# The flags of a stencil's four corners: one logical and over a hand-written access pattern in place of two comparisons

## The chip, the cores and the metric

The kernel runs on one NeuronCore of a Trainium2 chip. The metric is the device time of one execution in microseconds (us), lower is better. Beside the time there is a profile of one execution: a record of every instruction on TensorE (PE, and PEld for its weight loads), VectorE (DVE), ScalarE (ACT), GpSimd (POOL) and SyncE (SP), with starts, durations and what each waited for.

## The reference

The reference is a block of three parts on an input of 4 images of 32 x 32 pixels and 128 channels: a deformable convolution, an attention over the 1024 tokens of each image, and a mixture of experts with two experts for each image. Only the first part touches the change. Cut to that:

```python
offset = x1 @ off_w + off_b                      # 8 groups x 9 points x (x, y) for each pixel
mask = softmax((x1 @ mask_w + mask_b).reshape(N, H, W, 8, 9), -1)
loc = ref + grid * 1.0 + offset / norm           # where each of the 9 points is read
samples = bilinear_sample(img, 2.0 * loc - 1.0)  # four corners of the pixel cell, zero outside
out = (samples * mask).sum(-1)                   # 9 points, weighted
x = x + out @ out_w + out_b                      # then attention and experts
```

## The kernel before

The image rows are worked on in eight chunks of four rows; a chunk has all four images in the 128 partitions, and 4 rows x 8 groups = 32 row-groups for each partition. The nine bilinear reads of a row-group are written as one stencil of 7 x 7 weights: each point q = (kx, ky) puts an outer product of five "hat" weights in y and five in x at its place (ky, kx) in the 7 x 7 window. The hats lie in `hats` [128, 2, 288, 5]: axis 0 is x, axis 1 is y, then 32 row-groups x 9 points, then five taps. The y hats are multiplied by the softmax weight (`weigh_hats`, L1539).

A 7 x 7 stencil would have 49 taps. The four corner taps are left out: the kernel works with 45 (`NEAR`), and where a corner's weight isn't zero, that point counts as "far" and is fetched one by one by GpSimd. So for each row-group and each of the four corner points (kx, ky in {0, 2}) a flag says whether both the outermost x hat and the outermost y hat of that point are above zero. These flags are `at_corner` [128, 32, 2, 2], bf16. They are made on VectorE in `corners` (L1541 to L1551). TensorE sums them over the partitions, together with signs of the offsets, in `count_far` (L894 to L907, the flags in L903); the counts go to a list of far points (`list_far`, L1642) and to GpSimd.

The order of the work on VectorE is written out by hand. After a first part for chunk 0, `turn(k, ...)` runs for k = 0 to 6: it multiplies the shifted rows of chunk k with its stencil (`products`, L1656, 26 instructions for a chunk, each of 1024 or 512 elements for a partition), and between these products it prepares chunk k+1: the softmax (L1510 to L1529), `weigh_hats`, `corners`, and `stencils`, which for the points q = 0 to 8 makes an outer product (L1588) and adds it into the stencil (L1597). For 10 of the 32 row-groups the addition is done by TensorE instead (`sum_point`, L921), and since all nine points use one buffer `outer`, the outer product of point q >= 2 waits until TensorE has summed point q-1 (L1587, semaphore `outer_read`).

TensorE goes through the taps of chunk k one by one (`add_up`, L934, four transposing matmuls for each tap, waiting for `prod_done`), and between them it has nine convolution steps of chunk k+2 (L864), `count_far` (L902 to L905), the point sums (L921), the offsets of chunk k+2 (L856) and the output projection of chunk k-1 (L953 to L956). The buffer `prod` has seven slots, freed by `prod_free`. At the end of a turn ScalarE copies TensorE's point sums into the stencil (L600), and the first product of the next chunk waits for that.

There are eight calls of `corners`: one ahead of the turns for chunk 0, and one in each of the seven turns. In a turn it stands between `weigh_hats` (it waits for its result) and the outer product of point 0; it also waits for the far counts of the chunk before (`far_mm`).

## Time and profile before

| | |
|---|---|
| device time, three runs | 670.16 us median (669.46 to 671.59) |
| profiled execution | 669.48 us, of which 667.6 us from the first to the last instruction |
| granted TensorE clock, mean | 0.968 |
| TensorE matmul busy | 601.7 us (90%) |
| VectorE busy | 550.1 us (82%) |
| ScalarE busy | 235.1 us (35%) |
| GpSimd busy | 316.1 us (47%) |

In the profile a line L12 is line 12 of the kernel. A group of instructions is shown as line, engine, operation, output <- inputs, number, busy time and mean duration. "Idle before" is the time in which the engine stood still just before the instruction, with what ended it. The clock that the profile shows for TensorE is a share of 2.4 GHz: 1.00 is 2.4 GHz and 0.50 is 1.2 GHz. Matmul ends are modelled by the profile. The seven turns lie between 64.3 and 394.0 us; the attention and the experts follow them.

### The profile page before, as it was taken

Reading aid. Unit: us, or ns where it says so; the run is one execution under the profiler, and the core shown is the slowest. Engines: PE = TensorE matmul, PEld = TensorE weight load, DVE = VectorE, ACT = ScalarE, POOL = GpSimd, SP = SyncE. Lnnn points to the kernel's source line nnn. Section 1 sums busy time; section 2 is a strip of 40 time slices with the busy share of each in tenths; the row PEclk is TensorE's granted clock in tenths of the full one; section 3 lists DMA queues with packets and bytes.
Section 4 is the critical chain, followed back from the end, with each engine's and each line's share of the span. In section 5 each row is a group of like instructions: output and inputs, shape, how many; then the busy total and the mean of one; then the engine's idle time right before and its main releaser. Section 6 shows DMA issues by size and latency. Waiting matters only on the chain.

```text
span 667.6 us, 11041 instructions
## 1 busy us (share of the span) xinstructions
PE 601.7 (90%) x3634; PEld 444.3 (67%) x3634; DVE 550.1 (82%) x1028; ACT 235.1 (35%) x351; POOL 316.1 (47%) x408
## 2 busy tenths in 40 slices
PE   5989979979989989899797789999999999979995
PEld 4566656657667667576585567777777777765774
DVE  4668998999999999999999989757767766654877
ACT  6063504405307116126044000344454444415331
POOL 7604775786688588748578700202212211215222
PEclk9789989989989989989997999999999999999998
DMA  7087502103003007000000000000000000004111
GB/s 187 18 325 241 163 0 81 35 2 111 1 3 112 1 2 278 1 1 2 1 2 3 0 1 1 0 2 0 1 1 1 1 1 1 0 9 120 48 33 47
DMA packets 26243, 30.75 MB, mean 46 GB/s; under 512 B 5573, under 2 KB 18325, under 8 KB 26197
## 3 DMA queue, kind: packets, MB, share of 16 engines
q1 hardware_dynamic: 24094, 29.77, 13.6%
q0 software_dynamic: 1408, 0.36, 0.6%
q8 instruction: 29, 0.48, 0.3%
q14 instruction: 18, 0.14, 0.1%
q10 hardware_dynamic: 694, 0.01, 0.1%
HBM read 25.07 MB, written 5.05 MB: 45 GB/s over the span
## 4 chain that ended last, share of the span: by engine, by line
PE 58%; DVE 27%; issue 10%; ACT 3%; DMA 1%; DVEq 0%; POOL 0%; SPq 0%; ACTq 0%; POOLq 0%
DVE prod L1656 12%; PE banks L934 11%; PE banks L1061 9%; PE pair L1041 8%; DVE outer L1588 5%; PE pair L1129 4%; PE banks L1051 4%; PE pair L864 4%; PE banks L1167 4%; PE pair L856 2%; PE banks L921 2%; PE banks L956 2%; DVE stencil L1597 2%; DVE hats L1539 2%; ACT hats L624 1%
## 5 line engine op out<-in xcount | busy, mean ns | idle before, releaser
L934 PE MATMUL banks<-ident,prod 128*128 128x128 f32 x1440 | 203.6, 282 | 34.8 <-DVE prod L1656 33.7
L934 PEld LDWEIGHTS banks<-ident,prod 128*128 128x128 f32 x1440 | 165.4, 143 | 91.2 <-DVE prod L1656 64.9
L1656 DVE TENSOR_TENSOR prod<-shifted,stencil 128x1024 f32<-128x1024 f32 (+1 forms) x208 | 218.0, 1082 | 5.2 <-ACT stencil L600 3.5
L1412 POOL TENSOR_TENSOR rstd_now<-mv_now,neg_half 128x2 f32<-128x2 f32 x32 | 22.9, 716 | 127.4 <-DVE mv_now L1704 127.4
L864 PE MATMUL pair<-xg,dw_diag 128*128 128x512 f32 x144 | 74.6, 620 | 1.4 <-DVE xg L1466 1.4
L1307 POOL DMA_INDIRECT got<-padded,cell_now x44 | 57.8, 1314 | 19.0 <-issue 10.1
L1061 PEld LDWEIGHTS banks<-shifted 128*128 128x128 f32 x512 | 60.2, 192 | 8.1 <-issue 6.1
L1061 PE MATMUL banks<-shifted 128*128 128x128 f32 x512 | 63.3, 277 | 2.3 <-ACT shifted L740 1.4
L1588 DVE TENSOR_TENSOR outer<-hats 128x800 f32<-128x800 f32 x56 | 55.7, 995 | 6.2 <-PE banks L921 6.2
L1041 PE MATMUL pair<-shifted 128*128 128x512 f32 x128 | 60.6, 596 | 0.1
L1719 DVE TENSOR_REDUCE neg_max<-pair 128x1 f32<-128x1024 f32 x32 | 39.2, 1224 | 23.1 <-PE pair L1041 22.0
L624 ACT ACTIVATE hats<-off,tap_bias 128x576 f32<-128x576 f32 (+1 forms) x40 | 49.9, 1345 | 0.8
L735 ACT ACTIVATE shifted<-pair,neg_max 128x1024 f32<-128x1024 f32 x32 | 35.7, 1114 | 32.8 <-DVE neg_max L1719 32.7
L1597 DVE TENSOR_TENSOR stencil<-stencil,outer 128x550 f32<-128x550 f32 x56 | 41.6, 743 | 2.0
L646 ACT ACTIVATE xg<-banks 128x512 f32<-128x512 f32 (+1 forms) x8 | 4.8, 598 | 104.4 <-PE banks L941 104.4
L921 PE MATMUL banks<-outer,ident 128*128 128x250 f32 x116 | 37.4, 405 | 3.2 <-DVE outer L1588 3.2
L1724 DVE COPY shifted<-banks 128x512 f32<-128x512 f32 x32 | 22.0, 689 | 15.3 <-PE banks L1051 15.3
L1418 POOL TENSOR_TENSOR res<-res,bias_all 128x256 f32 x16 | 11.7, 728 | 46.2 <-DVE xg L1710 46.2
L1051 PE MATMUL banks<-ident,shifted 128*128 128x128 f32 x256 | 33.2, 273 | 0.3 <-ACT res L702 0.3
L1041 PEld LDWEIGHTS pair<-shifted 128*128 128x128 f32 x128 | 21.8, 190 | 15.9 <-issue 15.3
L864 PEld LDWEIGHTS pair<-xg,dw_diag 128*128 128x128 f32 x144 | 24.4, 201 | 11.4 <-issue 11.4
L1129 PE MATMUL pair<-shifted,stage 128*128 128x512 f32 x64 | 29.3, 597 | 2.3 <-DMA stage<-in_L_ffn_W_dram 2.3
(260 smaller groups left out, 957.3 us busy)
## 6 DMA issues: line engine op xcount, KB each, us to landing
shifted<-padded SPq DMA_DIRECT2D x42, 256.0 KB, 4.1
shifted<-padded SPq DMA_DIRECT2D x14, 640.0 KB, 8.2
res<-in_x_dram SPq DMA_DIRECT2D x4, 512.0 KB, 6.2
padded<-stage SPq DMA_DIRECT2D x4, 512.0 KB, 11.1
stage<-in_L_ffn_W_dram SPq DMA_DIRECT2D x16, 128.0 KB, 2.2
out_dram<-res SPq DMA_DIRECT2D x16, 128.0 KB, 1.8
got<-padded,cell_now POOLq DMA_INDIRECT x44, 2.9
padded<-stencil SPq DMA_DIRECT2D x2, 228.0 KB, 2.6
```

The costliest lines, as they stand in the source:

```text
L624: own(sc.activation(hats[:, :, :, t].rearrange("p a (r g) -> p a r g", r=ROWS), off[:, bass.ds(k % OFFS, 1), :, 0:2 * GP].rearrange("p s r ...
L864: mm = pe.matmul(conv_bank.rearrange("c (r a) -> c r a", r=ROWS), dw_diag[:, t, :], src, start=(t == 0), stop=(t == 8))
L921: pe.matmul(summed.rearrange("p (g a b) -> p g a b", a=WIN, b=WIN)[:, :, ky:ky + TAPS, kx:kx + TAPS], ident[:, :], src, start=False, stop= ...
L934: mm = pe.matmul(acc_of(c, r), prod[:, slot, r * G:(r + 1) * G, :].rearrange("p g c -> p (g c)"), ident[:, :], is_transpose=True, start=(t ...
L1041: mm = pe.matmul(pair[s][:, h * 512:(h + 1) * 512], keyed[:, bass.ds(i * P, P)], normed_t[:, bass.ds((i // TILES) * TOK + h * 512, 512)], ...
L1051: mm = pe.transpose(bank[h][:, m * P:(m + 1) * P], probs[:, s, (4 * h + m) * P:(4 * h + m + 1) * P], ident[:, :])
L1061: mm = pe.matmul(bank[2][:, 0:C], probs_t[:, m * P:(m + 1) * P], normed[:, bass.ds((i // TILES) * TILES + m, 1), :].rearrange("p t c -> p ...
L1129: pe.matmul(pair[j][:, (f % 2) * 512:(f % 2 + 1) * 512], w1_sel[:, 2 * (q // 2) + j, (f % 2) * P:(f % 2 + 1) * P], normed2_t[:, q * 512:(q ...
L1307: gp.indirect_dma_start(out=got[:, j, a, :], out_offset=None, in_=table, in_offset=bass.IndirectOffsetOnAxis(ap=cell_now[:, j, a:a + 1], a ...
L1588: ve.tensor_tensor(to if q == 0 else outer[:, :, :, :], hy[:, :, q, :].unsqueeze(3).to_broadcast(full), hx[:, :, q, :].unsqueeze(2).to_bro ...
L1597: own(ve.tensor_tensor(to, to, outer[:, 0:DIRECT, :, :], ALU.add))
L1656: ins = ve.tensor_tensor(prod[:, dx:dx + n, :, :], shifted[:, dx:dx + n, bass.ds(((c % HALF) * ROWS + dy) * G, ROWS * G), :], stencil_of[: ...
```

## The change

In `corners`, two instructions are replaced by one. Before, for each of the two point columns kx a SCALAR_TENSOR_TENSOR of 64 elements (32 row-groups x 2 point rows) compares the x hat with zero and the result with the y hat: (hx <= 0) < hy, which is one where both are above zero. After, one TENSOR_TENSOR of 128 elements takes the logical and of the x hats and the y hats. The two point columns and two point rows have different steps in `hats` (in x 34 and 10 elements, in y 30 and 14), which the pattern helper of the language doesn't give in one slice; so a small function writes the access pattern by hand. The output is the same [128, 32, 2, 2] of bf16, now written in one piece. The waits ahead of it and the semaphore behind it stay as they are.

```diff
+        def outermost(axis, per_column, per_row):
+            first = hats[:, axis, :, :].rearrange("p (g q) t -> p g (q t)", q=PTS)[:, :, 0:1]
+            return bass.AP(tensor=first.tensor, offset=first.offset,
+                           ap=[first.ap[0], first.ap[1], [per_column, 2], [per_row, 2]])
...
-                at = hats[:, :, :, :].rearrange("p a (g q) t -> p a g (q t)", q=PTS)
-                for kx in range(2):
-                    x0, y0 = (2 * 3 * TAPS + TAPS - 1) * kx, 2 * 3 * TAPS * kx
-                    last = ve.scalar_tensor_tensor(at_corner[:, :, kx, :], at[:, 0, :, x0:x0 + 2 * TAPS + 1:2 * TAPS], 0.0,
-                                                   at[:, 1, :, y0:y0 + 3 * TAPS:2 * TAPS + TAPS - 1], ALU.is_le, ALU.is_lt)
+                last = ve.tensor_tensor(at_corner[:, :, :, :], outermost(0, 2 * 3 * TAPS + TAPS - 1, 2 * TAPS),
+                                        outermost(1, 2 * 3 * TAPS, 2 * TAPS + TAPS - 1), ALU.logical_and)
                 last.then_inc(corners_done, 1)
```

On VectorE, in the first turn, the stretch around the flags stands so before the change (row: line, operation, output <- inputs, shape, semaphores waited for):

```order
L1529 TENSOR_TENSOR off<-mask,row_sum 128x4x72 [waits dve]
L1656 TENSOR_TENSOR prod<-shifted,stencil 128x512 [waits prod_free]
L1539 TENSOR_TENSOR hats<-hats,off 128x1440 [waits hats_done,dve]
L1549 SCALAR_TENSOR_TENSOR at_corner<-hats 128x32x2 [waits dve,far_mm]
L1549 SCALAR_TENSOR_TENSOR at_corner<-hats 128x32x2
L1588 TENSOR_TENSOR stencil<-hats 128x32x5x5 [waits dve,stencil_clear]
```

The same stretch of VectorE in the changed kernel, whose lines are numbered a little higher:

```order
L1534 TENSOR_TENSOR off<-mask,row_sum 128x4x72 [waits dve]
L1658 TENSOR_TENSOR prod<-shifted,stencil 128x512 [waits prod_free]
L1544 TENSOR_TENSOR hats<-hats,off 128x1440 [waits hats_done,dve]
L1551 TENSOR_TENSOR at_corner<-hats 128x128 [waits dve,far_mm]
L1590 TENSOR_TENSOR stencil<-hats 128x32x5x5 [waits dve,stencil_clear]
```

Nothing has moved: in this place and in the seven others two rows have become one, with the waits of the first. The order on the other engines is the same.

## Rows read from the trace of the kernel before

**Rows 1.** The page's costliest groups: taps on TensorE and products on VectorE.
```profile
L934 PE MATMUL banks<-ident,prod 128*128 128x128 f32 x1440 | 203.6, 282 | 34.8 <-DVE prod L1656 33.7
L1656 DVE TENSOR_TENSOR prod<-shifted,stencil 128x1024 f32<-128x1024 f32 (+1 forms) x208 | 218.0, 1082 | 5.2 <-ACT stencil L600 3.5
```

**Rows 2.** Windows, turns 0, 2, 4, 5, 6: length, busy PE, PEld, DVE, ACT, POOL; PEclk.
```profile
64.29:111.61 47.32, 41.41 (x236) 29.15 (x235) 45.06 (x53) 16.92 (x18) 30.00 (x42) 0.93 0.23 74
...
158.81:206.01 47.20, 43.19 (x263) 31.34 (x262) 44.93 (x54) 15.76 (x18) 34.01 (x35) 0.96 0.14 41
...
253.57:301.25 47.68, 43.21 (x263) 31.25 (x261) 45.57 (x53) 15.73 (x18) 32.03 (x40) 0.96 0.26 98
301.25:347.11 45.86, 41.37 (x259) 29.66 (x258) 45.16 (x54) 15.72 (x18) 33.06 (x39) 1.00 0.01 2
347.11:394.00 46.89, 36.46 (x246) 28.59 (x245) 44.64 (x53) 10.27 (x12) 29.28 (x33) 0.93 0.02 2
```

**Rows 3.** Groups of VectorE by shape: count, then busy us, mean ns, idle before.
```profile
L1588 DVE TENSOR_TENSOR outer<-hats 128x800 f32<-128x800 f32 x56 | 55.7, 995 | 6.2 <-PE banks L921 6.2
...
L1500 DVE SCALAR_TENSOR_TENSOR gate<-gate,conv 128x512 f32<-128x512 f32 x8 | 5.5, 682 | 4.5 <-ACT conv L591 4.5
...
L1466 DVE TENSOR_SCALAR xg<-xg,gn_v 128x864 f32<-128x864 f32 x4 | 4.1, 1117 | 0.0
...
L1549 DVE SCALAR_TENSOR_TENSOR at_corner<-hats 128x64 bf16<-128x64 f32 x16 | 3.8, 280 | 1.3 <-DVE hats L1539 1.2
...
L1513 DVE TENSOR_TENSOR mask<-off,row_max 128x288 f32<-128x288 f32 x8 | 3.6, 456 | 0.0
...
L1837 DVE TENSOR_SCALAR stage<-stage,weight_all 128x256 f32<-128x256 f32 x8 | 2.4, 345 | 0.0
...
L1466 DVE TENSOR_SCALAR xg<-xg,gn_v 128x160 f32<-128x160 f32 x4 | 1.5, 440 | 1.2 <-POOL gn_v L1227 1.2
...
L1784 DVE TENSOR_SCALAR route<-route,route_s 4x8 f32<-4x8 f32 x1 | 0.2, 219 | 0.0
...
L1794 DVE SCALAR_TENSOR_TENSOR route<-route 4x8 f32<-4x8 f32 x1 | 0.2, 154 | 0.0
```

**Rows 4.** VectorE in order of time (start, duration): chunk 0, turns 1, 2, 6.
```profile
54.82 0.99 DVE L1612 TENSOR_TENSOR prod<-hats 128x800 f32<-128x800 f32 x1 [1.72 <-PE banks L921]
...
128.70 0.99 DVE L1588 TENSOR_TENSOR outer<-hats 128x800 f32<-128x800 f32 x1
...
152.37 0.99 DVE L1588 TENSOR_TENSOR outer<-hats 128x800 f32<-128x800 f32 x1 [0.85 <-PE banks L921]
...
169.64 0.47 DVE L1549 SCALAR_TENSOR_TENSOR at_corner<-hats 128x64 bf16<-128x64 f32 x2 [0.18 <-DVE hats L1539]
170.02 0.98 DVE L1588 TENSOR_TENSOR stencil<-hats 128x800 f32<-128x800 f32 x1
...
176.00 0.98 DVE L1588 TENSOR_TENSOR outer<-hats 128x800 f32<-128x800 f32 x1
...
364.23 1.03 DVE L1588 TENSOR_TENSOR outer<-hats 128x800 f32<-128x800 f32 x1
```

**Rows 5.** TensorE in order of time: point sums and waits of the same turns.
```profile
128.01 0.59 PE L921 MATMUL banks<-outer,ident 128*128 128x250 f32 x2
...
151.68 0.59 PE L921 MATMUL banks<-outer,ident 128*128 128x250 f32 x2
...
175.23 0.59 PE L921 MATMUL banks<-outer,ident 128*128 128x250 f32 x2
...
182.59 2.23 PE L934 MATMUL banks<-ident,prod 128*128 128x128 f32 x16 [1.21 <-DVE prod L1656]
...
362.56 1.04 PE L921 MATMUL banks<-outer,ident 128*128 128x250 f32 x2
```

**Rows 6.** Windows of TensorE, in turns 2 and 5: length, busy, granted clock.
```profile
191.00:195.00 4.00, 4.00 (x19) 0.57 0.04 4
...
330.00:343.00 13.00, 11.38 (x77) 1.00 0.00 1
```

## The prediction

> **What bounds the kernel now.** I read the page first: its costliest groups are the taps on TensorE and the products on VectorE, and each waits for the other: TensorE stood idle 33.7 us for VectorE's products, VectorE hardly at all in front of a product [rows 1]. Both belong to the seven turns, so the turns were cut out as windows [rows 2]. A turn takes 45.9 to 47.7 us and VectorE is busy 44.6 to 45.6 us of it. It is the fuller engine, and the instructions that the change touches stand in its stream. Eight times 2 flags instructions take 16 x 280 ns [rows 3], under 4.5 us in all. So this is a question of a fraction of a microsecond for each turn, and whether it arrives at the end depends on what else is nearly late at that place.
>
> That was read from the order of time in turn 2. The pair of flags instructions starts at 169.64, the next instruction at 170.02 [rows 4]: the pair holds VectorE for 0.38 us. From there VectorE runs without a gap to point 2's outer product at 176.00. That one needs TensorE's sum of point 1, which stands at 175.23 and lasts 0.59, so until 175.82 [rows 5]. How long after such a sum VectorE can start is seen where it did wait: the sum at 151.68 ends at 152.27 and the outer product behind it starts at 152.37 [rows 4, 5], 0.10 us later. So at 176.00 only 0.08 us are free. TensorE works without a gap through its convolution steps before that sum, and it was released by the first products of the turn, ahead of the flags. **A VectorE that comes earlier to this place will meet TensorE's sum.** Behind it things are loose again: TensorE stands 1.21 us for a product at 182.59 [rows 5].
>
> **The change, part by part.** *Removed:* eight pairs of 64-element instructions. Each pair costs 0.38 us from its start to the next start. With 280 ns an instruction this says that the next one starts about 0.09 us before the end of the one before it (0.28 - 0.19).
>
> *Added:* eight instructions of 128 elements, a form that the trace doesn't have. Three rows bound it.
> - Dense: a TENSOR_TENSOR of 800 elements takes 995 ns, one of 288 takes 456 [rows 3], so 1.05 ns for an element and 153 ns fixed. At 128 elements this gives 288 ns, and to the next start 0.20 us. Saving: 0.38 - 0.20 = 0.18 us a turn.
> - With the price for scattered elements that the old form pays. Dense SCALAR_TENSOR_TENSORs take 154 ns at 8 elements and 682 at 512 [rows 3], so 64 dense elements would take 213. The flags take 280, 67 ns more. If this is paid for each element (1.05 ns more), the new one takes 288 + 128 x 1.05 = 422 ns, to the next start 0.33. Saving: about 0.05 us a turn.
> - The same 67 ns paid once for an instruction: 288 + 67 = 355 ns, to the next start 0.27. Saving: 0.11 us.
>
> Which? The two forms of the input's normalisation (L1466) step 16 bytes from element to element: 440 ns at 160 and 1117 at 864, 0.96 ns for an element. The dense TENSOR_SCALARs take 219 ns at 8 and 345 at 256, 0.51 for an element [rows 3]. So scattered elements cost more one by one, not once, and the flags' steps are wider still, both before and after. I take the second row, **0.05 us saved in each turn**, and keep 0.18 as the upper end. The lower end is below nothing: one instruction as long as the two old ones without their overlap, 0.56 - 0.09 = 0.47, loses 0.09 a turn; nothing in the trace excludes it, though it would need a price for an element that no row shows.
>
> The Trainium skill has a rule that speaks against this change (Advanced Engine Details and Errata, SBUF Cachelines): SBUF is read in lines of 16 bytes, and accesses that each fall in another line pay for it. The 67 ns above agree with it, and by it the saving is the 0.05 us. It also has a formula that speaks for it (VectorE: DVE Perf Modes, The TRN2 errata): (N + 151) / 0.96 ns for an fp32 tensor_tensor, so an estimated 291 ns here, and the saving would be the 0.18 us. The old pair's row doesn't fit that formula (224 by it, 280 measured), which is why I don't go by it.
>
> *What reaches the end.* `corners` for chunk 0 lies in the first part: VectorE there waits 1.72 us for TensorE at 54.82 [rows 4], and TensorE came to that sum over its convolution steps, which don't need the flags. That wait covers the whole pair: worth nothing. In the seven turns the gain is the smaller of the saving and the room in front of point 2's outer product. The room is start of the outer product less end of the sum less 0.10. In turn 1 the sum ends at 128.60 and the outer product starts at 128.70: none. In turn 2: 0.08. In turn 6 the sum ends at 363.60 and the outer product starts at 364.23 [rows 4, 5]: 0.53. The same two instructions in turns 0, 3, 4 and 5 give 0.02, 0.27, 0.10 and 0.12. With 0.05 a turn: 0.02 + 0 + 5 x 0.05 = **0.27 us**. With 0.11: 0.02 + 0 + 0.08 + 0.11 + 0.10 + 0.11 + 0.11 = 0.53. With 0.18: 0.02 + 0 + 0.08 + 0.18 + 0.10 + 0.12 + 0.18 = 0.68. With a loss of 0.09 all of it counts: 7 x 0.09 = 0.63 lost.
>
> The flags' own reader, TensorE's `count_far`, comes well behind in its stream, after the sum of point 1; that the flags are ready sooner is worth nothing. The change adds no wait, and the one instruction waits for the same two semaphores. GpSimd and ScalarE have no step less or more.
>
> *The sum.* The profiled execution took 669.48 us, 667.6 of them between first and last instruction; less 0.27 is 669.21. This execution was 0.68 under the median of the three runs, 670.16. Against the median: 670.16 - 0.27 = 669.9. About 0.3% (2.0 us) is what a measurement of this kernel can tell from no change; the whole pair, eight times, holds 3.0 us.
>
> **Rivals.**
>
> *All of it arrives.* The new instruction is dense in its price, and TensorE's point sums turn out not to hold VectorE (matmul ends are modelled, and 0.1 us may be the model's). Then 7 x 0.18 = 1.26 us: 668.9. For: VectorE shows no gap at point 2 now. Against: the 0.10 us repeats wherever it did wait, and the flags' 280 ns.
>
> *The clock moves, faster.* In turn 2 TensorE's granted clock lies at 0.57 between 191 and 195, most of it at 1.2 GHz, right behind a stretch in which it waited again and again for products; in turn 5, with the same waits, it stays at 1.00, 2.4 GHz [rows 6]. Turn 5 takes 45.86 us, turns 2 and 4 take 47.20 and 47.68 [rows 2]. So such a stretch costs 1.3 to 1.8 us, and turns 0 to 4 all have one, by their granted clock under 1.00. A small shift of the waits decides it, and this change shifts them. One stretch fewer: 670.16 - 0.27 - 1.6 = 668.3; two fewer: 666.7.
>
> *The clock moves, slower.* The same mechanism on the other side, in turn 5: it is the one turn of the first six without a slow stretch. If TensorE's waits between 325 and 333 us fall so that the clock goes to 1.2 GHz there, turn 5 becomes like turn 4: + 1.6, so 670.16 - 0.27 + 1.6 = 671.5. It decides as soon as the stretch reaches the part from 333 us on, where TensorE runs without a gap and sets the pace. For: the waits in turn 5 are as long as in the others. Against: the change can only shorten TensorE's waits, by at most the room counted above.
>
> *It saves nothing.* The one instruction holds VectorE as long as the pair, or up to 0.09 us a turn longer: 670.2 to 670.8. For: it moves the same 128 scattered elements of each of two inputs. Against: the fixed part of an instruction, about 150 ns, is paid once in place of twice.
>
> **How the numbers follow.** Forecast as above, with a gain of 0.27 to 0.68: 0.60. All of it arrives: 0.08. Clock faster: 0.13. Clock slower: 0.12. It saves nothing: 0.07. The predicted time is the forecast's, 669.9. The range, 668.3 to 671.3: it holds the forecast and the full gain with what runs of the same kernel differ by (the three lie over 2.1 us), the case of no saving, about half of the faster clock's cases and half of the slower's; 2 in 10 are left out. Faster by over 0.3% (under 668.1) needs two slow stretches fewer, or one with a low measurement: 0.06. Slower by over 0.3% (over 672.2) needs a slow stretch more and a high measurement: 0.04. The rest is no difference: 0.90.
>
> **What would show it.** In the changed kernel the flags' instruction: 422 ns shows the price of scattered elements, 355 a price for the instruction, 288 none. From its start to the next start: 0.33, 0.27 or 0.20 us, against 0.38. The idle time of the outer products that wait for TensorE's sums, 6.2 us in all now [rows 3], should grow by what doesn't arrive: about 0.1 us at 0.05 a turn, 0.6 at 0.18, and the new waits should stand in front of point 2 in turns 0 and 1. The turns' windows: 47.2 us with a slow stretch, 45.9 without; if the number of slow stretches differs, the time goes with it and not with the flags. The prediction is wrong if the time falls by over 1 us with the same number of slow stretches, or if the new instruction holds VectorE longer than the pair.

## The result and the profile after

The changed kernel took 666.24 us (median of 22 executions, 663.62 to 670.17), the kernel before, run beside it, 669.78 (22 executions, 666.11 to 676.31). The ratio is 0.9947, 95% interval 0.9924 to 0.997: faster by 0.5%. Ratios here leave out the few executions over 1.5% above the fastest of their kernel, and in the later sets they are not the quotient of the two medians. The time forecast was 669.9 with a range from 668.3 to 671.3, so the time lies outside it. The profiled execution took 665.69 us, 663.8 of them from the first to the last instruction, at a mean granted clock of 0.974 (before: 667.6 and 0.968).

The groups that answer to [rows 1] and [rows 3], from the page of the changed kernel (line, engine, operation, number, busy us, mean ns, idle before):

```profile
L939 PE MATMUL banks<-ident,prod 128*128 128x128 f32 x1440 | 202.7, 282 | 35.6 <-DVE prod L1658 34.2
...
L1658 DVE TENSOR_TENSOR prod<-shifted,stencil 128x1024 f32<-128x1024 f32 (+1 forms) x208 | 218.7, 1085 | 5.2 <-ACT stencil L605 3.5
...
L1590 DVE TENSOR_TENSOR outer<-hats 128x800 f32<-128x800 f32 x56 | 55.6, 993 | 5.2 <-PE banks L926 5.1
```

The flags among the groups of VectorE by shape, and VectorE and TensorE in order of time in turn 0:

```profile
L1551 DVE TENSOR_TENSOR at_corner<-hats 128x128 bf16<-128x128 f32 x8 | 2.8, 346 | 1.3 <-DVE hats L1544 1.2
```
```profile
72.53 0.34 DVE L1551 TENSOR_TENSOR at_corner<-hats 128x128 bf16<-128x128 f32 x1 [0.17 <-DVE hats L1544]
72.79 0.98 DVE L1590 TENSOR_TENSOR stencil<-hats 128x800 f32<-128x800 f32 x1
...
76.49 2.35 DVE L1658 TENSOR_TENSOR prod<-shifted,stencil 128x1024 f32<-128x1024 f32 x2
78.90 0.99 DVE L1590 TENSOR_TENSOR outer<-hats 128x800 f32<-128x800 f32 x1
```
```profile
78.20 0.59 PE L926 MATMUL banks<-outer,ident 128*128 128x250 f32 x2
```

The new instruction takes 346 ns (its mean; 343 to 353 in five further profiles with all eight of them, 358 in e1_pad, and 391 in e18_ends_after, where one of the eight took 617) and holds VectorE from 72.53 to 72.79, 0.26 us, where the pair held it 0.38: 0.12 us saved in a turn. Point 2's outer product comes to TensorE's sum as forecast: the sum of point 1 ends at 78.79 and the outer product starts 0.11 us behind it, as where it waited before. Nothing in these rows is worth more than a microsecond. The windows are: length, TensorE busy, granted clock, DMA share, GB/s for the part ahead of the turns (the lead), turns 0 to 6, and the rest.

```profile
0.00:61.81 61.81, 51.22 (x236) 0.94 0.58 192
61.81:107.75 45.94, 40.02 (x236) 0.96 0.25 82
107.75:153.35 45.60, 40.79 (x253) 1.00 0.15 43
153.35:200.79 47.44, 43.24 (x264) 0.96 0.13 41
200.79:248.43 47.64, 43.18 (x263) 0.96 0.13 40
248.43:296.02 47.59, 43.23 (x263) 0.96 0.26 98
296.02:341.88 45.86, 41.51 (x259) 1.00 0.01 2
341.88:390.44 48.56, 38.01 (x246) 0.89 0.02 2
390.44:663.80 273.36, 256.77 (x1634) 0.99 0.06 16
```

The same windows of the kernel before, as far as [rows 2] don't have them (lead, turns 1 and 3, rest):

```profile
0.00:64.29 64.29, 53.62 (x236) 0.92 0.57 188
...
111.61:158.81 47.20, 42.41 (x254) 0.96 0.15 42
...
206.01:253.57 47.56, 43.34 (x262) 0.96 0.13 40
...
394.00:667.60 273.60, 256.74 (x1634) 0.99 0.06 16
```

Of the 3.80 us between the two profiles 2.48 lie in the lead, 1.38 in turn 0, 1.60 in turn 1; turns 2 to 5 are 0.23 longer (188.30 and 188.53), turn 6 is 1.67 longer, the rest 0.24 shorter. Each of the larger steps goes with the granted clock: lead 0.92 to 0.94, turn 0 0.93 to 0.96, turn 1 0.96 to 1.00, turn 6 0.93 to 0.89. From the mean clocks, (1 - 0.968) x 2 x 667.6 = 42.7 us were at 1.2 GHz before and (1 - 0.974) x 2 x 663.8 = 34.5 after. **The time went with the clock**, and the largest piece, the lead's, was lost on TensorE where no flags had been made yet. These are the windows of 38 to 46 us, first of before, then of the changed kernel; the first flags start at 45.95 and 45.12:

```profile
38.00:46.00 8.00, 6.49 (x30) 0.79 1.00 413
```
```profile
38.00:46.00 8.00, 6.50 (x28) 1.00 1.03 404
```

TensorE's second run of convolution steps, which starts ahead of the flags and doesn't need them, first of before, then of the changed kernel:

```profile
43.38 8.35 PE L864 MATMUL pair<-xg,dw_diag 128*128 128x512 f32 x18
```
```profile
41.36 7.89 PE L869 MATMUL pair<-xg,dw_diag 128*128 128x512 f32 x18
```

It starts 2.02 us earlier in the changed kernel and ends 2.48 us earlier (49.25 and 51.73), the whole difference of the lead. On VectorE only 0.83 us of it stands ahead of the flags; the whole stands there after its wait for TensorE, 1.72 us before [rows 4] and 0.45 after, which ends at 54.82 and 52.34.

### The profile page after: what moved, and what is told of

The parts are those of the page before. It is cut to its first block, busy times and chain, and to the rows that moved or that the text cites. A ratio compares the mean times of both kernels' runs of the same rounds, so it can differ in the third digit from the quotient of the medians.

```text
span 663.8 us, 11033 instructions
## 1 busy us (share of the span) xinstructions
PE 598.0 (90%) x3634; PEld 441.0 (66%) x3634; DVE 550.1 (83%) x1020; ACT 235.0 (35%) x351; POOL 318.5 (48%) x408
## 4 chain that ended last, share of the span: by engine, by line
PE 55%; DVE 29%; issue 10%; ACT 2%; DMA 1%; SPq 0%; DVEq 0%; POOL 0%; ACTq 0%; POOLq 0%
DVE prod L1658 14%; PE banks L939 10%; PE banks L1066 8%; PE pair L1046 8%; DVE outer L1590 5%; PE pair L1134 4%; PE banks L1056 4%; PE pair L869 4%; PE banks L1172 4%; PE banks L926 2%; PE pair L861 2%; DVE stencil L1599 2%; DVE hats L1544 2%; PE banks L961 1%; DMA res<-in_x_dram 1%
## 5 line engine op out<-in xcount | busy, mean ns | idle before, releaser
L869 PE MATMUL pair<-xg,dw_diag 128*128 128x512 f32 x144 | 73.1, 609 | 0.3 <-DVE xg L1471 0.3
L1312 POOL DMA_INDIRECT got<-padded,cell_now x44 | 60.9, 1384 | 19.0 <-issue 10.1
L1056 PEld LDWEIGHTS banks<-ident,shifted 128*128 128x128 f32 x256 | 29.3, 141 | 1.7 <-ACT res L707 0.7
```

The source lines that it names most:

```text
L869: mm = pe.matmul(conv_bank.rearrange("c (r a) -> c r a", r=ROWS), dw_diag[:, t, :], src, start=(t == 0), stop=(t == 8))
L1056: mm = pe.transpose(bank[h][:, m * P:(m + 1) * P], probs[:, s, (4 * h + m) * P:(4 * h + m + 1) * P], ident[:, :])
L1312: gp.indirect_dma_start(out=got[:, j, a, :], out_offset=None, in_=table, in_offset=bass.IndirectOffsetOnAxis(ap=cell_now[:, j, a:a + 1], a ...
```

## The experiments

The theory after the result: the flags' instructions give about half a microsecond, and the rest is a smaller share of time at 1.2 GHz. The rivals: the 0.12 us a turn arrive in a larger measure than the order of time shows; or the difference is chance, of the chip or of the executions drawn. In the table "ratio" is to the kernel before on the same chip (five further groups of runs, with 22 to 35 executions of before each, whose medians are 668.93 us for e1 to e4, 669.72 for e5 to e8, 671.29 for e9 to e12, 668.48 for e13 to e16 and 668.74 for e17 and e18).

| run | what | median us (range, n) | ratio [95%] |
|---|---|---|---|
| e1_pad | after, hold given back | 669.06 (665.3-673.7, 12) | 0.9995 [0.9965, 1.0025] |
| e2_two_ands | after, two ands of 64 | 670.04 (664.7-674.4, 12) | 1.000 [0.9969, 1.0031] |
| e3_keep_before | before, clock held in the turns | 665.36 (660.8-672.9, 12) | 0.9933 [0.9896, 0.997] |
| e4_keep_after | after, clock held in the turns | 663.73 (660.5-665.8, 10) | 0.9907 [0.9876, 0.9939] |
| e5_no_flags | flags left out | 667.21 (663.9-668.9, 12) | 0.9925 [0.9893, 0.9957] |
| e6_three | before, a third comparison | 670.46 (667.2-672.8, 12) | 0.9995 [0.9963, 1.0027] |
| e7_after_again | after, repeated | 669.85 (664.2-670.9, 12) | 0.997 [0.9937, 1.0002] |
| e8_first_turns | new form in chunks 0 to 2 | 668.49 (665.0-669.9, 12) | 0.9956 [0.9927, 0.9985] |
| e9_last_turns | new form in chunks 3 to 7 | 665.64 (662.8-669.6, 12) | 0.9922 [0.9893, 0.9951] |
| e10_hold_before | before, clock held throughout | 662.62 (658.2-665.7, 6) | 0.9878 [0.9834, 0.9922] |
| e11_hold_after | after, clock held throughout | 662.67 (657.6-664.2, 6) | 0.988 [0.9835, 0.9925] |
| e12_after_third | after, repeated | 665.79 (664.1-668.3, 11) | 0.9931 [0.9904, 0.9958] |
| e13_tail_before | before, experts' wait filled | 668.86 (665.1-670.8, 12) | 0.9992 [0.9961, 1.0022] |
| e14_tail_after | after, experts' wait filled | 668.91 (665.8-670.8, 12) | 0.9985 [0.9957, 1.0013] |
| e17_ends_before | before, lead and experts' wait filled | 664.91 (661.8-667.7, 12) | 0.9962 [0.994, 0.9984] |
| e18_ends_after | after, lead and experts' wait filled | 666.01 (664.0-667.6, 12) | 0.9957 [0.993, 0.9984] |

### The flags' instruction and its time on VectorE

e1_pad lets one small dummy follow the new instruction, so that VectorE is held as long as by the old pair:

```diff
+                ve.tensor_tensor(gn_stats[...], ident[:, 0:48], ident[:, 0:48], ALU.mult)
```

> The changed kernel with one more VectorE instruction of 48 elements, on a buffer that nothing reads then, right behind the flags (about 0.11 us by the line of the dense TENSOR_TENSORs), so that VectorE is held as long as by the old pair. Theory 1, clock: the change made VectorE 0.12 us earlier in each turn, and this decides how often TensorE falls to 1.2 GHz; then the time goes back to about 669.8 us. Theory 2, direct: the 0.12 us of each turn add up and nothing else; then 666.2 + 7 x 0.11 = 667.0 us. Theory 3, something else in the changed program than VectorE's time: 666.2 us.

e2_two_ands makes the logical and in two instructions of 64 elements:

```diff
-                last = ve.tensor_tensor(at_corner[:, :, :, :], outermost(0, ...), outermost(1, ...), ALU.logical_and)
...
+                for kx in range(2):
...
+                    last = ve.tensor_tensor(at_corner[:, :, kx, :], at[:, 0, :, x0:...], at[:, 1, :, y0:...], ALU.logical_and)
```

> The logical and, but as two instructions of 64 elements over the old slices: the operation changed, the number of instructions not. If the price of scattered elements is paid once for an instruction, one of them takes about 275 ns and the pair holds VectorE about 0.37 us, as before; if for each element, 248 ns and 0.32 us. Theory 1, clock: about 669.5 us, near the kernel before. Theory 2, direct: 666.2 + 7 x 0.11 = 667.0 us. A theory that the operation itself matters: 666.2 us.

VectorE of e1_pad in order of time (the same place as above), and the flags' group of e2_two_ands:

```profile
72.34 0.34 DVE L1551 TENSOR_TENSOR at_corner<-hats 128x128 bf16<-128x128 f32 x1 [0.17 <-DVE hats L1544]
72.60 0.21 DVE L1554 TENSOR_TENSOR gn_stats<-ident 128x48 f32<-128x48 f32 x1
72.72 0.98 DVE L1591 TENSOR_TENSOR stencil<-hats 128x800 f32<-128x800 f32 x1
```
```profile
L1554 DVE TENSOR_TENSOR at_corner<-hats 128x64 bf16<-128x64 f32 x16 | 3.8, 278 | 1.3 <-DVE hats L1544 1.2
```

In both VectorE is held about 0.38 us again (here 72.34 to 72.72), by an and with a dummy or by two ands, and both take the time of before: 0.9995 and 1.000. So what counts in the change is one instruction in place of two, not the operation: an and of 64 elements takes 278 ns, a compare of 64 took 280 [rows 3]. But 0.12 us in eight chunks is 0.96 us at the most, and the difference was 3.5. e6_three goes the other way, with a third comparison into an unused tile; e5_no_flags leaves the flags out and hands out zeros that are set once at the start:

```diff
-                for kx in range(2):
+                for kx in range(3):
+                    to = at_corner[:, :, kx - 1, :] if kx else mv[:, :, :]
+                    kx = max(kx - 1, 0)
...
-                    last = ve.scalar_tensor_tensor(at_corner[:, :, kx, :], ...
+                    last = ve.scalar_tensor_tensor(to, ...
```

> The kernel before with a third comparison of 64 elements into a buffer that nothing reads then: VectorE is held 0.57 us by the flags in place of 0.38. Directly 7 x 0.19 = 1.3 us more at most. Theory 1 in its simple form: slower than the kernel before by 1 to 3 us. If any shift only draws the slow stretches anew: between 664 and 672.

```diff
+            own(gp.memset(at_corner[:, :, :, :], 0.0))
...
-                last = ve.tensor_tensor(at_corner[:, :, :, :], outermost(0, ...), outermost(1, ...), ALU.logical_and)
-                last.then_inc(corners_done, 1)
+                ve.sem_inc(corners_done, 1)
```

> The flags are left out: at_corner is set to zero once at the start, so points whose corner weight isn't zero lose that corner; VectorE has no flags instruction, 0.26 us a turn less than in the changed kernel. Directly this may bring at most the room in front of point 2's outer product that is left, under 0.6 us over all turns. Theory 1 in its simple form (the earlier VectorE, the fewer slow stretches): 663 to 665 us. If instead any shift only draws the slow stretches anew: somewhere between 664 and 670, without order.

A third comparison, which holds VectorE 0.58 us, costs nothing that shows (0.9995; 1 to 3 us more were expected by the simple form of the theory, that an earlier VectorE has fewer slow stretches), and without flags nothing more is gained that the runs can tell (0.9925, the interval overlaps with those of the changed kernel). The time doesn't follow the length of the flags in proportion: the kernels that hold VectorE for 0.38 us or longer in every chunk lie at 1.000, those with 0.26 us or nothing at 0.9925 to 0.997. e8_first_turns and e9_last_turns use the new form in a part of the chunks (this is e8; e9 has k > 2 in the first line):

```diff
+                if k <= 2:
+                    last = ve.tensor_tensor(at_corner[:, :, :, :], outermost(0, ...), outermost(1, ...), ALU.logical_and)
+                else:
+                    for kx in range(2):
+                        last = ve.scalar_tensor_tensor(at_corner[:, :, kx, :], ..., ALU.is_le, ALU.is_lt)
```

> The new form for chunks 0 to 2 alone (ahead of the turns and in turns 0 and 1), the old pair in turns 2 to 6. In the two profiles the changed kernel had one slow stretch fewer in each of turns 0 and 1 and as many in the others up to turn 5. Theory 1, with the gain in these two turns: about 666.5 us, and turns 0 and 1 at 45.6 to 45.9 us or one slow stretch less than before. If the gain is spread over all turns: about 668.5 us.

> The old pair for chunks 0 to 2, the new form in turns 2 to 6 alone. If the gain lies in turns 0 and 1: as the kernel before, 669 to 670 us. If what counts is where VectorE and TensorE stand at the end of the turns: executions above 671 us go away, as with the new form in all turns.

Five of the eight chunks alone give at least as much as all of them (0.9922 and 0.9947), and three alone 0.9956, with an interval that reaches to 0.9985. A saving that adds up chunk by chunk would make the two together equal to the whole. They make 1.2%, where the three sets of the whole change gave 0.3 to 0.7%. The two repeats of the changed kernel belong here:

> The changed kernel as it is, on the chip of this call, beside the next three. Theory 1, clock: about 666 us where the kernel before takes 669 to 670; the time goes with the mean granted clock, 0.974 against 0.968 to 0.970. If the 3.5 us were a matter of the chip or of the day: no difference here. In the turns without a slow stretch the length stays 45.6 to 45.9 us.

> The changed kernel as it is, a third time. The executions so far fall in two groups, 664 to 668 and 670 to 671 us, and the share of the groups differed between two chips (16 of 22 in the lower one, then 4 of 12). If the change makes a stable gain, the median is 666 to 667; if the groups are a draw: anywhere between 666 and 670, and no execution above 671, where the kernel before has three in ten.

One gave 0.997, its interval just holding no change and its median (669.85 us) no lower than that of before beside it (669.72); the other gave 0.9931. In e7_after_again 4 of 12 executions lie at 664 to 667 us and 8 at 669.6 to 670.9; in the first set 16 of 22 lay under 668. It is the same program with two times, in shares that differ from one set to the next. In every set the executions at a higher clock tend to be the shorter ones: of the 22 executions of the first set those at a clock of 0.980 took 663.6 and 664.3 us, those at 0.974 between 665.7 and 667.7, those at 0.970 about 670.

### The clock held

e3_keep_before and e4_keep_after put seven dummy matmuls at three places in each turn, in waits of TensorE:

```diff
+                    if i == first_of(POINT_UNIT[4]) + 1:
+                        pe.wait_ge(res1_done, max(k, 1))
+                        keep_clock(7, bank[0])
...
                         sum_point(k + 1, point_taps.index(i))
+                        if point_taps.index(i) in (3, 5):
+                            pe.wait_ge(res1_done, max(k, 1))
+                            keep_clock(7, bank[0])
```

> The kernel before, with seven dummy matmuls on TensorE at three places of each turn where it waits for VectorE (behind the sums of points 3 and 5 and one tap behind that of point 4), into a bank that is free there. Theory 1, clock: TensorE keeps 2.4 GHz in the turns, each slow stretch saved gives 1.3 to 1.8 us, four or five of them: 662 to 664 us, with a mean granted clock above 0.98. Theories 2 and 3: no gain, 669.8 us or a little more, since the dummies do nothing.

> The changed kernel with the same dummy matmuls. Theory 1, clock: the same as the kernel before with them, within 0.7 us, since only the direct gain is left: 661.5 to 663.5 us. Theories 2 and 3: 3.5 us under the kernel before with the dummies.

Windows of e3_keep_before: turns 0 and 1 together, then 2 to 5, and the rest behind the turns; the same of e4_keep_after below it.

```profile
63.63:155.14 91.51, 87.88 (x572) 1.00 0.21 63
155.14:201.25 46.11, 45.73 (x305) 1.00 0.14 42
201.25:247.61 46.36, 45.74 (x304) 1.00 0.13 41
247.61:294.65 47.04, 45.84 (x305) 1.00 0.27 100
294.65:340.49 45.84, 45.52 (x301) 1.00 0.01 2
...
387.11:665.60 278.49, 261.54 (x1634) 0.97 0.06 16
```
```profile
64.32:155.81 91.49, 87.87 (x572) 1.00 0.20 61
155.81:201.81 46.00, 45.62 (x305) 1.00 0.14 42
201.81:248.02 46.21, 45.59 (x304) 1.00 0.13 41
248.02:294.92 46.90, 45.80 (x305) 1.00 0.27 100
294.92:340.71 45.79, 45.48 (x302) 1.00 0.01 2
...
388.69:662.00 273.31, 256.75 (x1634) 0.99 0.06 16
```

Here the clock is 1.00 in the first six turns of both, so the flags' own effect can be read: 0.02 us in turns 0 and 1, then 0.11, 0.15, 0.14 and 0.05, together **0.47 us**. Turns 0 and 1 give nothing, as the order of time of before had said. This rests on one profile of each. Holding the clock is worth far more: before gets 3.6 us faster by it (668.93 to 665.36), though not the 662 to 664 us expected. The 1.6 us by which e4_keep_after's median is lower than e3_keep_before's are more than the flags' own time: e3's executions fall in two groups, six at 660.8 to 663.3 us and six at 667.5 to 672.9, and its profile is one of the second group, with 278.49 us behind the turns in place of 273. Why no execution of e4 has that longer end is not shown.

e10_hold_before and e11_hold_after hold the clock throughout, with dummies in the group norm, the input projection, fewer at each of the three places in a turn, the last turn and the router:

```diff
-            keep_clock(1, pair[0][:, 512:1024])
+            keep_clock(7, pair[0][:, 512:1024])
...
+                        keep_clock(4, bank[0])
+                    if not conv_ahead and i == point_taps[0]:
+                        pe.wait_ge(res1_done, max(k, 1))
+                        keep_clock(9, bank[0])
...
+                            keep_clock(5, bank[0])
...
-            keep_clock(20, bank[1])
+            keep_clock(25, bank[1])
```

> The kernel before with dummy matmuls at all the places where TensorE waits and a slow stretch followed in the profiles: four or five at the three places of each turn, nine ahead of point 0's sum in the last turn, more in the group norm and the input projection, and more at the router ahead of the experts. Theory 1, clock: the granted clock stays near 1.00 (0.99 and above) and the time falls to 655 to 660 us, with little spread between executions.

> The changed kernel with the same dummy matmuls. With the clock held on both sides, what is left between this and the kernel before with dummies is the change's direct gain: 0.3 to 0.6 us by the room in front of point 2's outer product. If the difference stays at 3 us, the clock isn't the way by which the change works.

The two medians are 662.62 and 662.67 us, of six executions each: with the clock held, the old and the new flags take the same time as far as these tell, and both are 1.2% faster than before, more than the change itself gives. The profile of e11_hold_after is the shortest of all, 655.9 us from the first to the last instruction at a mean clock of 0.998. Turn by turn the new form is shorter there by -0.14 us in turns 0 and 1 together, 0.20, 0.08 and 0.14 in turns 2, 3 and 5, together 0.28; the same turns gave 0.33 in e4_keep_after. The executions still spread from 657.6 to 665.7 us, where 655 to 660 with little spread was expected, and the profile of e10_hold_before, its longest execution, shows one cause. Its turn 4 and TensorE's wait there:

```profile
243.18:297.69 54.51, 47.76 (x292) 0.94 0.23 86
```
```profile
282.92 1.12 PE L943 MATMUL banks<-ident,stage 128*128 128x128 f32 x4 [5.72 <-POOLq L1419]
```

In e11_hold_after the same turn takes 46.74 us. Here TensorE waited 5.72 us for GpSimd's far points, and the clock fell about the end of that wait. The wait doesn't need the held clock: in e6_three, without dummies, TensorE waits 3.75 us for GpSimd in turn 4, which takes 51.30 us.

### The two ends

The executions over 671 us came only with before (53 of 158) and with kernels that hold VectorE for the pair's 0.38 us or longer in every chunk (e1, e2, e3 and e6); of 45 of the changed kernel there was none, nor of the 36 of e5, e8 and e9. Two profiles, of e2_two_ands and e3_keep_before, have 278 to 280 us behind the turns. TensorE there, first e2_two_ands (busy times of PE, PEld, DVE, ACT, POOL, then the clock), then e3_keep_before, then a third profile of before, e15_before_look:

```profile
599.00:602.00 3.00, 3.00 (x8) 1.42 (x7) 1.19 (x4) 1.38 (x2) 0.00 (x0) 0.50 0.46 130
```
```profile
596.00:605.00 9.00, 9.00 (x21) 4.42 (x20) 2.06 (x5) 2.75 (x4) 0.05 (x1) 0.51 0.47 119
```
```profile
596.00:605.00 9.00, 7.14 (x38) 4.42 (x37) 4.34 (x22) 4.00 (x7) 0.00 (x0) 1.00 0.43 107
```

Just ahead of this stretch the first expert matmul waits 1.5 to 2.3 us for the expert's weights, here in e2_two_ands and in e15_before_look:

```profile
597.45 2.63 PE L1134 MATMUL pair<-shifted,stage 128*128 128x512 f32 x4 [1.86 <-DMA stage<-in_L_ffn_W_dram]
```
```profile
600.28 1.98 PE L1129 MATMUL pair<-shifted,stage 128*128 128x512 f32 x4 [1.86 <-DMA stage<-in_L_ffn_W_dram]
```

e13_tail_before and e14_tail_after fill that wait:

```diff
-            keep_clock(20, bank[1])
+            keep_clock(31, bank[1])
```

> The kernel before with 31 in place of 20 dummy matmuls ahead of the first expert matmul, so that TensorE has work in most of its wait for the expert's weights (1.5 to 2.3 us in the profiles so far); nothing else is changed. Theory (the executions over 671 us are those with a stretch at 1.2 GHz behind that wait, as in the profiles of e2_two_ands and e3_keep_before, and they come with either form): of 112 executions of the kernel before 40 lay over 671 us; here at most one in ten does, the median is that of the other 72, 668.6 us, ratio about 0.996 to 0.998. Rival (they come from the turns): 3 to 4 in ten stay over 671 us, ratio 1.00.

> The same 31 dummies in the changed kernel. Theory: its executions over 668.5 us (14 of 45 so far, about 670.1) are the same stretch at the experts, so they go and the median is that of the other 31, 666.0 us; against e13_tail_before the changed form then still gains 2.6 us (0.4%), since the turns' share is left alone. Rival (the change acted on the experts' wait alone): the two kernels are equal within 0.5 us. Second rival (the slow executions come from the turns): a third stays at about 670 us.

In e13_tail_before no execution of 12 lies over 671 us (7 of 23 of before on the same chip did), which speaks for the theory; its median, 668.86, is near the 668.6 expected, but before's own was 668.48 on this chip, and the ratio, 0.9992, is not the 0.996 to 0.998 expected. The second half of the theory fell: the changed kernel with its experts' wait filled has its executions at about 670 us still (5 of 12), so those come from elsewhere, and it gained nothing on e13_tail_before (668.91 and 668.86), as both rivals had it. The changed kernel without dummies wasn't run beside these two, nor beside e17 and e18, so it is not shown that it would have been faster than before there.

e15_before_look and e16_before_look are profiles of before, unchanged:

> The kernel before unchanged, for the profile of one more execution. Theory: if it lies over 671 us, its granted clock is 0.50 for 6 to 8 us behind the first expert matmul (about 600 us) and the part behind the turns takes 278 to 280 us; if it lies under 671 us, that part takes 273 to 274 us. Rival: an execution over 671 us has its extra time in the turns, 330 us or more, with the part behind them at 273 to 274.

> The kernel before unchanged once more, for another draw: the same two readings as for e15_before_look. The turns take 325 to 328 us with 3 to 6 of the first six at a granted clock under 1.00; a kernel whose draw were fixed by its instructions would show the same turns as the first profile of before (only turn 5 at 1.00).

They took 668.01 and 668.70 us and repeat the first profile of before place by place: the lead at 0.92, turns 2 to 4 at 0.96, turn 5 at 1.00, turn 6 at 0.93, and in e16_before_look all seven turns within 0.17 us of their first length. So the pattern of a program can come again in other executions. It need not: the three profiles of the changed kernel differ in their turns (turns 0 and 1 take 91.54, 91.32 and 94.05 us, turn 5 is at 1.00, 1.00 and 0.96), and the executions of before spread over 12 us. No profile of an execution of before over 671 us was caught, so that these have their extra time behind the turns rests on the runs with the wait filled alone (none over 671 us of 24 in e13 and e17).

The three profiles of the changed kernel have a lead of 61.7 to 61.9 us at 0.94, the three of before 63.8 to 64.3 at 0.92. The flags' form in chunk 0 doesn't decide that: e4_keep_after and e8_first_turns have the new form there and 0.79 in the window of 38 to 46 us like before, e6_three and e9_last_turns the old form and 1.00. What goes with it stands earlier still, in the group norm. These are the windows of 14.0 to 15.7 us of the first profile of before and of the changed kernel:

```profile
14.00:15.70 1.70, 1.30 (x6) 1.00 0.78 222
```
```profile
14.00:15.70 1.70, 1.15 (x6) 0.84 0.68 189
```

In all sixteen profiles without added dummies in the lead a stretch at 1.2 GHz begins about here (15.7 to 24 us: 0.59 to 0.66). The clock is still at 1.00 up to 15.7 us in all seven that have the slow stretch at 38 to 46 us (three of before, e3, e4, e8 and e13), and it has fallen by then (0.67 to 0.93) in eight of the nine without that stretch; the ninth, e14_tail_after, is at 1.00. Both forms of the flags are on both sides. So the two kinds of lead differ some 30 us ahead of the first flags, and it is not the time of the flags in that execution that makes the difference. Why all three profiles of before are of one kind and all three of the changed kernel of the other is open. e17_ends_before and e18_ends_after hold the lead and the experts' wait and leave the turns alone:

```diff
-            keep_clock(2, pair[0][:, 512:1024])
+            keep_clock(6, pair[0][:, 512:1024])
...
+                if q == 6:
+                    keep_clock(6, bank[3])
...
-            keep_clock(20, bank[1])
+            keep_clock(31, bank[1])
```

> The kernel before with dummy matmuls ahead of the turns only (in the waits of the group norm and the input projection, where its profiles show two stretches at 1.2 GHz, at 15 to 23 and 40 to 45 us) and the 31 ahead of the first expert matmul; the turns are left alone. Theory (of the 3.8 us between the first profiles of before and after, 2.5 lie ahead of the first flags instruction and 1.4 in turn 0 behind it, so the gain is mostly there): the part ahead of the turns falls from 66.0-66.6 to 62-64 us without a stretch at 40 to 45, the median is 664 to 666, ratio 0.992 to 0.996. Rival (the gain is in turns 1 to 6): the median stays within 1 us of e13_tail_before's kind, ratio 0.998 to 1.00.

> The same dummies in the changed kernel, turns left alone. Theory: with both ends held the two kernels differ by the turns alone, at most one stretch and the direct 0.46 us: 0 to 1.5 us less than e17_ends_before, 663 to 665 us. Rival (the change acts through the turns' clock): 2.5 us or more less than e17_ends_before. Second rival (the change acts nowhere but through chance): equal within 0.5 us.

Windows of e17_ends_before (lead, turns 0 and 1 together, turns 2, 3 and 4), then of e18_ends_after (lead, turns 0 and 1, turn 4).

```profile
0.00:59.77 59.77, 53.17 (x272) 1.00 0.60 198
59.77:151.06 91.29, 79.89 (x487) 1.00 0.21 63
151.06:197.02 45.96, 41.77 (x262) 1.00 0.14 42
197.02:244.72 47.70, 43.23 (x263) 0.96 0.13 40
244.72:292.45 47.73, 43.05 (x261) 0.96 0.26 98
```
```profile
0.00:60.03 60.03, 53.41 (x272) 1.00 0.60 197
60.03:152.95 92.92, 81.53 (x488) 0.98 0.21 62
...
246.13:295.20 49.07, 44.62 (x263) 0.93 0.26 95
```

Before with its ends held takes 664.91 us, a little less than the changed kernel without (666.24, in another set of runs). In its profile turns 0 to 2 run at 1.00, though nothing in them was touched; but this profile is of the shortest of its twelve executions (661.77 us, mean clock 0.987; the others are at 0.974 to 0.982). The changed kernel with the same dummies takes 666.01 us, no less. With the same lead at 1.00 its turns 0 and 1 are at 0.98 and turn 2 at 0.96, and its turns fell at other places, turn 4 at 0.93 and 49.07 us. So in this setting the new flags bring nothing that can be measured, and the runs show no better pattern of the clock in the turns for either form.

**What follows.** Shown: the flags' own gain is about half a microsecond of the 3.5; the rest goes with the granted clock; and in four pairs with the clock held at some places (turns, throughout, experts, both ends) the new form has no lead over the old one that the runs can tell from none. Not settled: why the changed program, left alone, comes out faster by 0.5 and 0.7% in two sets of three (0.3% in the third, which can't be told from none), with no execution over 671 us, and why e1_pad and e2_two_ands don't, whose lead in the profiles is the shorter one too. That the shifts of 0.1 us themselves choose the pattern in the turns was not shown step by step, and in the lead no instruction of the change runs ahead of the difference.

## Why the prediction was wrong, point by point

The step that failed is that the sum left the granted clock as it was and gave a faster clock a chance of 0.13. Of the 3.5 us by which the time fell, about 0.5 are the flags' and the other 3 went with the clock. The price of the new instruction was wrong as well, but that is worth only a quarter of a microsecond.

**The bound and the place: right.** The flags stand in the fuller engine's stream, point 2's outer product meets TensorE's sum, and where the clock was held turns 0 and 1 give 0.02 us, as counted.

**The price of the new instruction: the wrong row of three.** 422 ns was taken, 346 measured, 0.26 us to the next start and not 0.33: the second candidate (355 and 0.27). The step that failed is "scattered elements cost more one by one, not once". It came from two forms that step 16 bytes (L1466); the flags' own rows speak otherwise: from 278 ns at 64 elements (e2_two_ands) to 346 at 128 is 1.06 ns for an element, the dense price, so their extra is paid once. e2_two_ands had been put at 275 ns by that reading, and at 248 by the other. The Trainium skill's rule (Advanced Engine Details and Errata, SBUF Cachelines), that an access in another line each time pays for it, does not show here as a price for each element; the measurement decides. By the Trainium skill's formula for fp32 (VectorE: DVE Perf Modes, The TRN2 errata) 64 and 128 elements would take an estimated 224 and 291 ns; both rows lie above it by 54 and 55, a constant, so its slope agrees with the runs and its fixed part doesn't for this pattern.

**The direct gain: right but for the price.** With the second price the prediction's own sum is 0.53 us for seven turns, 0.42 of them in turns 0 to 5; with the clock held these gave 0.47. The forecast's 0.27 is half of that; the miss is 0.04% of the time.

**The idle time in front of the outer products** was to grow by what doesn't arrive. It fell from 6.2 to 5.2 us. The row stands almost wholly in turns with a slow stretch: 1.1 to 1.3 us in each of turns 0 to 4 before; after the change none in turns 0 and 1, and 1.7 in turn 6. In e3_keep_before and e4_keep_after it is 0.5 and 2.0, and the difference lies in turn 6 (0.96 and 0.93). In kernels whose clock differs this row says nothing on the flags.

**The clock rival: the right mechanism and price in the turns, the wrong weight.** "Two fewer" was put at 666.7 us; measured 666.24. In the profiles turns 0 and 1 lost a stretch each and gave 2.98 us where 3.2 had been counted. That the whole comes so near is partly luck: the lead is 2.48 us shorter and turn 6 1.67 longer, and neither was in the count. The failed step is the chance: 0.13 for a faster clock and 0.06 for faster by over 0.3%. Three things were left out. The count of stretches took in turns 0 to 5 alone; the lead, turn 6 and the part at the experts change too, and the lead holds the largest piece. The rival was thought of as a step at one turn, while here the lead, turns 0, 1 and 6 changed at once. And three executions over 2.1 us were taken for the spread: 158 executions of before lie between 664.8 and 676.8 us, and the medians of its six sets between 668.48 and 671.29. A range of 3 us around one median was too narrow: before's own medians fill it.

**The test that was named for it held.** "If the number of slow stretches differs, the time goes with it and not with the flags": the granted clock of lead and turns says that it did.

## What to carry to other kernels

Where the granted clock in the profile goes up and down, look at the windows of the whole span first and ask how much lies at 1.2 GHz; if that costs more than the change (here 8.7 us by the medians against 0.5), the forecast is about the clock and needs a range as wide as it. To measure a small change in such a kernel, hold the clock in both versions with dummy matmuls in TensorE's waits and compare those; and if holding it gains more than the change, as here (1.2% against 0.5%), that is the change to make. One instruction over a hand-written pattern in place of two is worth the fixed part of an instruction less the overlap with the next one, here 0.12 us each time, and no more.

## What the runs showed of the hardware

- The profiles of one program can repeat its slow stretches place by place (three of before) or differ (three of the changed kernel, turns 1, 2 and 5), and timed executions of one program fall in groups about 4 us apart (e7_after_again).
- Of TensorE's clock: a stretch at 1.2 GHz in the group norm stands at slightly different places from profile to profile, and with its place goes whether another one follows at 40 us (clock at 14.0 to 15.7 us and at 38 to 46 us: 1.00 and 0.79 in seven profiles, 0.67 to 0.93 and 1.00 in eight, 1.00 and 1.00 in one).
- In e2_two_ands and e3_keep_before the clock fell to 0.50 for ten microseconds or more behind waits of 1.86 and 2.17 us for the expert's weights, though TensorE then had work without a gap; in e15_before_look and before it stayed at 1.00 behind waits of 1.86 and 2.34 us, so the length of the wait doesn't decide it. With the wait filled no execution of 24 lay over 671 us (e13, e17), where 13 of 46 of before did beside them.
- For a scattered 128-partition operation on VectorE the extra over a dense one did not grow with the elements: 278 ns at 64, 346 at 128.
